# Moving the shared expert's units from between the routing links to beside the zero rows and the sends

## The reference, cut to what matters

```python
h = layernorm(x) * (1 + cb) + sb
logits = h @ gate_w.T                      # 64 experts
probs = softmax(logits); top 6, weights normalised
routed = sum over the 6 of  w * (silu(h @ w1[e].T) @ w2[e].T)      # inner size 176
g, u = split(h @ shared_gate_up.T)                                 # inner size 352
shared = (silu(g) * u) @ shared_down.T
x = x + gb * (routed + shared)
```

## Time and profile before

| | us |
|---|---|
| median of 3 runs | 1748.65 (1747.83 to 1749.74) |
| the profiled execution | 1739.2 |
| its span | 1737.0 |
| granted TensorE clock, mean | 0.927 |
| busy: PE, DVE, ACT, POOL | 1492.1, 1347.0, 975.6, 738.9 |

### The profile page before, as it was taken

How to read it: one execution, slowest core, us unless ns; L and a number is a source line. 1 busy time by engine, 2 the same in 40 slices (tenths; PEclk the granted TensorE clock), 3 DMA queues, 4 the chain that set the end, 5 groups by cost and what they waited for, 6 DMA issues and landing times. The chain is left out here.

```text
span 1737.0 us, 29842 instructions
## 1 busy us (share of the span) xinstructions
PE 1492.1 (86%) x9504; PEld 1136.9 (65%) x9504; DVE 1347.0 (78%) x2154; ACT 975.6 (56%) x1732; POOL 738.9 (43%) x578
## 2 busy tenths in 40 slices
PE   5789999889999769999887999969179999999921
PEld 4566666566766546666565677647169999999910
DVE  2669889678899578888759889954359999999966
ACT  3456766457566445656353556624148878778700
POOL 0434334543437733335843343820525555445510
PEclk6899999999999989999998999989689999999965
DMA  3011121011113111122201222310979989988754
GB/s 127 1 55 55 55 64 50 16 55 55 56 55 104 43 34 49 55 61 74 95 19 37 64 56 64 102 41 1 250 225 289 291 275 292 290 286 277 225 181 157
DMA packets 111089, 198.99 MB, mean 115 GB/s; under 512 B 17481, under 2 KB 63063, under 8 KB 110816
## 3 DMA queue, kind: packets, MB, share of 16 engines
q1 hardware_dynamic: 94048, 167.49, 31.3%
q0 software_dynamic: 12288, 25.41, 4.1%
q10 hardware_dynamic: 4608, 4.26, 0.9%
HBM read 160.96 MB, written 44.50 MB: 118 GB/s over the span
## 5 line engine op out<-in xcount | busy, mean ns | idle before, releaser
L1499 POOL TENSOR_TENSOR ssq<-ssq,ysq 128x512 f32<-128x512 f32 x128 | 165.6, 1293 | 448.7 <-ACT ysq L930 448.1
L1114 DVE SCALAR_TENSOR_TENSOR e<-bank,scal,e 128x511 f32<-128x511 f32 (+2 forms) x384 | 286.4, 746 | 27.8 <-ACT e L925 18.7
L1572 POOL DMA_INDIRECT outputs<-hsw,x_rows x160 | 190.5, 1190 | 216.6 <-DVE hsw L1444 207.1
L437 PE MATMUL bank<-h_hi,wi_hi 128*128 128x512 f32 x512 | 246.8, 482 | 18.5 <-issue 14.4
L620 PE MATMUL bank<-e,wn 128*128 128x512 f32 x512 | 256.9, 625 | 1.0 <-DVE e L1179 1.0
L925 ACT ACTIVATE e<-bank,scal 128x512 f32<-128x512 f32 x128 | 99.6, 778 | 200.2 <-PE bank L439 200.2
L439 PE MATMUL bank<-h_hi,wi_lo 128*128 128x512 f32 x512 | 206.4, 403 | 0.0
L438 PE MATMUL bank<-h_lo,wi_hi 128*128 128x512 f32 x512 | 205.4, 401 | 0.0
L1049 DVE TENSOR_TENSOR ew_lo<-ew,ew_hi 128x864 fp32r<-128x864 f32 x160 | 169.3, 1058 | 46.1 <-ACT ew_hi L809 36.4
L1486 POOL TENSOR_TENSOR wi_lo<-wi,wi_hi 128x512 fp32r<-128x512 f32 x128 | 165.9, 1296 | 48.9 <-ACT wi_hi L809 48.9
L809 ACT ACTIVATE ew_hi<-ew 128x864 fp32r<-128x864 f32 x160 | 145.7, 911 | 49.9 <-DMA ew<-expert_w 49.9
(11 more groups left out here) (239 smaller groups left out, 3617.1 us busy)
## 6 DMA issues: line engine op xcount, KB each, us to landing
ew<-expert_w SPq DMA_DIRECT2D x160, 432.0 KB, 4.3
wi<-in_w SPq DMA_DIRECT2D x128, 256.0 KB, 2.7
x_rows<-grouped SPq DMA_DIRECT2D x160, 130.0 KB, 3.2
wo<-out_w SPq DMA_DIRECT2D x128, 128.0 KB, 2.3
got<-outputs SPq DMA_DIRECT2D x16, 768.0 KB, 4.3
grouped<-zeros_out SPq DMA_DIRECT2D x33, 130.0 KB
grouped<-zeros_out ACTq DMA_DIRECT2D x32, 130.0 KB
outputs<-hsw,x_rows POOLq DMA_INDIRECT x160, 4.9
```

The costliest lines, as they stand in the source:

```text
L437: mm(out, w_hi, x_hi, start=first, stop=False)
L1114: v.scalar_tensor_tensor(dst[:, d:], src[:, 0:SEQ - d], taps(TAPS - 1 - d), dst[:, d:], ALU.mult, ALU.add).then_inc(S[done], 1)
L1499: g_.tensor_tensor(ssq[:, :], ssq[:, :], ysq[:, :], ALU.add).then_inc(S["ssq_done"], 1)
L1572: g_.indirect_dma_start(outputs, bass.IndirectOffsetOnAxis(x_rows[:, i % XD, EMB:EMB + 1].bitcast(U32), 0), y_rows[:, i % YD, :], None, bo ...
```

## The change

Two tables of numbers change, no other line:

```diff
-GAP = 27
-SHARED_AT = (4, 6, 7, 8, 9, 10, 11, 13, 14, 18, 20, 22)
+GAP = 37
+SHARED_AT = (23, 25, 26, 27, 28, 29, 30, 31, 32, 33, 34, 35)
```

## The result

The changed kernel takes 1761.24 us (median of 4, 1760.16 to 1762.42), the kernel before beside it 1749.2 (1747.83 to 1750.15): a ratio of 1.007, 95% interval 1.0052 to 1.0087, some 12 us slower. The forecast was 1752.4, 3.7 us slower, with a range up to 1757.5. The sign was right and the size was not.

The account below looks back on a forecast made before the run. The expert part was bound by row lists, sends and, last, 65 zero-row transfers; chain -24.9, then ScalarE's loads +17.0, issue -4.5, landing -8.7 gave +3.7 us, 1740.7 of span, 1752.4 at the median, range 1748.5 to 1757.5.

Parts of the forecast that it names:

- The units: Shared-expert units behind the rows: 4.15 us each, 45.2 from first to last, so ScalarE's zero rows start 17.0 us later.
- The step to the median: Profiled execution 1742.9 us with the change; the median lies 9.45 above the profiled execution, moved unchanged: 1752.4.
- The rest of the sum: Chain -24.9, 8.3 behind the rank unchanged, ScalarE's zero-row issue -4.5 and landing -8.7 us.
- Rank: Rank matmuls in the routing chain, freed of the units, start at 1184.4 instead of 1209.27: 24.9 us earlier.
- rank to the first `hw_hi`: From the rank matmuls to the first unit's hw_hi on ScalarE: 8.3 us as before, so hw_hi at 1192.7.
- from the last `hw_hi` to the fill: ScalarE's 32 zero rows behind its last unit: 28.4 us to issue, 2.5 to land, 3.83 to the first filling matmul.
- the rival with the 2.4 GHz level: TensorE keeps 2.4 GHz through the whole routing chain: -10.6, so -6.9 us overall, 1741.7; chance 0.04.
- the one in which the clock rises inside the logits: 16 of the 24 logits steps cost 0.112 instead of 0.215: -1.6, so +2.1 us overall, 1750.8; chance 0.13.
- ScalarE's queue alone: ScalarE's 32 zero rows running alone: a group every 3.6 us, first load to last issue 28.4.
- the rival of 4.26 a group: ScalarE's zero-row queue is no faster alone: last issue 4.6 us later, +8.3 overall, 1757.0; chance 0.12.
- SyncE's half: SyncE's zero rows start behind fill_row at 1195.9, take 35 us and are issued by 1231, not late.
- The sign that I had named: Listed among the signs of a wrong forecast: a unit costing more than 4.3 us beside the sends and SyncE's transfers.

## Why the prediction was wrong, point by point

- **The failed step** is "The units": 4.15 us each, "ScalarE and DVE keep up with that pace in the trace". The trace showed it where no send lay beside. Beside the sends, on the slower kind of chip, the term is 67.8 us and not 45.2, since TensorE's signals reach ScalarE up to 21 us late.
- **The step to the median** failed with it. I saw that the profiled execution lay 9.45 us under the median and carried that over as a constant. By the profiles it lies in this very stretch, and it costs each order differently. From rank to fill: 58.9 and 71.9 us in the kernel before on a quicker and a slower chip (+13.1), 87.6 and 109.7 in the changed one (+22.1). The difference, 9.0, and the 2.8 by which the fill comes later on the quicker chip (1268.55 against 1265.80) make 11.8 of the 12.0 measured. The two profiles of slower chips themselves lie 13.8 apart at the fill, since their ranks are 24.0 apart and not 25.95, so the agreement is good to some 2 us.
- **Why the new order suffers more.** In the kernel before only idle engines and the issue of zero rows lie beside the sends. In the new one the units do, each of which needs TensorE's signal, and ScalarE's zero rows stand behind them; the sum of the stall goes straight to the end: 21.7 us more from the first `hw_hi` to the last (67.8 against 46.1 on the quicker chip), 22.1 more up to the fill. With the sends held back the stall is gone from the units. With all zero rows on SyncE the time is 13 us less, of which 9.4 remain without a stall.
- **The rest of the sum** held on the quicker chip, with errors that partly cancel. Rank 25.95 earlier (24.9 forecast); rank to the first `hw_hi` 8.64 (8.3); eleven units 46.14 (45.2); from the last `hw_hi` to the fill 32.8 (34.7): +2.8 against +3.7. The medians there are 6.6 apart, 4.0 to 8.0 by the interval; against the 3.7 some 3 us stay unexplained. Eight single executions of the changed kernel lie between 1738.3 and 1743.5 there.
- **The clock.** The chain ran at 0.50 from 1156 to 1180, and the mean took 3.80 (3.75 forecast): the rival with the 2.4 GHz level is out, and so is the one in which the clock rises inside the logits: they lay at 0.50 to their end (1176.8). The rank came 24.9 + 2.8 before its place in the earlier trace rows, and the 2.8 were there at the start of the mean.
- **ScalarE's queue alone** took 25.73 us from first to last (26.8 forecast), a group every 3.37, so the rival of 4.26 a group is out. SyncE's half took 48.74 where I had 35, harmless: it was done at 1242.9.
- **The sign that I had named** was the right one ("if a unit costs more than 4.3 us beside the sends"), but no rival with a price stood behind it, and so the range ended too early. The earlier trace rows showed what DMA transfers do beside the sends; nothing in them showed what signals do there.

So the forecast was also a matter of where it was measured: on the one quicker chip that ran both kernels as they are the changed one is 0.34% slower, and 0.7% where the result was taken.

## What to carry to other kernels

Before a row is taken as the price of a stretch, ask whether the profiled execution is like the median one; a gap of half a per cent has a place in the kernel, and the change may lie right on it. Sends by a list of rows should not follow each other without a pause where engines must hear from each other: two short operations behind every third took 14 to 22 us off three different orders on the slower chips. On a quicker chip the pauses were not tried by themselves. And a queue's work shouldn't stand behind an engine's loop that it doesn't need: 56 to 8 in place of 32 to 32 brought another 13 to 16 us (1739.4 to 1723.8, on two chips; 10.0 and 23.4 below their kernels before).

## What was not expected of the hardware

- On some chips, sends by row lists at one in 1.27 us slow most steps of SyncE's sequencer to some 0.69 us (29 ns for a move otherwise) and bring TensorE's signals up to 21 us late, while DMA engines are half idle. In the changed kernel it starts 3 to 7 us behind the first send and ends 4 to 5 us behind the last issue. Plain transfers from GpSimd at one in 0.54 us do not do it (moves of 29 ns).
- 16 bytes a row do it too: 10.07 us of wait in a Silu beside them alone. With paced sends right behind it lasted until 1241, 18 us beyond the last small one, and a signal of TensorE came 35 us late (1205.5 to 1241.0).
- The times of the kernel before fall into two kinds: 1747 to 1751 us on three chips, 1733 to 1734 on three others, 14 us apart. Traces show the stretch on the first three (on one of them only in kernels with pauses, and weak) and not on the other three. On which chips the result and the first profile were taken isn't known.
- Open: by what path it works. The Trainium skill (DMA: Bandwidth & Descriptors, "SWDGE vs HWDGE vs iDMA") says that transfers issued from GpSimd get their descriptors from a program on GpSimd. By that both the plain transfers and the sends have such a program behind them, and only the sends did harm, so this alone doesn't tell. No run here shows where the signals and the register moves are held up. Late instruction fetch was not tried either; from 1185 to 1235 the changed kernel's trace has three transfers of instructions, 0.2% of the DMA engines' time, and that of the quicker chip five, 0.4%.
